# Row moments of odd graph pairs moved from VectorE to ScalarE, and zero matmuls ahead of the first product

## What is computed

```python
h = jnp.maximum(_layernorm(x), 0.0); x = x + relation_layer(h, adj, Wq, Wk, Wv)
h = jnp.maximum(_layernorm(x), 0.0); x = x + graph_attention(h, W, a, beta, adj)
h = jnp.maximum(_layernorm(x), 0.0); x = x + normalised_adj @ (h @ weight) + bias
h = jnp.maximum(_layernorm(x), 0.0); x = x + masked_8_head_attention(h, adj, ...)
def _layernorm(x, eps=1e-05):
    m = mean(x, -1); v = var(x, -1)
    return (x - m) / sqrt(v + eps)
```

## Time and profile before

| | |
|---|---|
| median of 3 runs | 716.94 us (715.76 to 717.35) |
| the profiled execution, its own time | 716.58 us |
| its span in the profile | 714.8 us |
| PE busy | 692.3 us (97%) |
| PEld busy | 652.9 us (91%) |
| DVE busy | 627.9 us (88%) |
| ACT busy | 555.9 us (78%) |
| POOL busy | 462.1 us (65%) |

### The profile page before, as it was taken

The page is one execution under the profiler, slowest core; times in us unless marked ns, Lnnn a source line. Parts: engine busy times, 40 slices in busy tenths (PEclk is TensorE's granted clock), DMA queues, the critical chain, the costliest instruction groups (busy, mean ns, idle before and its releaser), DMA issues.

```text
span 714.8 us, 22548 instructions
## 1 busy us (share of the span) xinstructions
PE 692.3 (97%) x6938; PEld 652.9 (91%) x6938; DVE 627.9 (88%) x2618; ACT 555.9 (78%) x1892; POOL 462.1 (65%) x585
## 2 busy tenths in 40 slices
PE   5999999999999999999998999999999999999996
PEld 5999999999888888889997999999999999999994
DVE  5899888987799999699998999998889998899876
ACT  3665656565689999876665998889888988898895
POOL 2445454554587788588884776776677666766662
DMA  8222310000000000000000000000000000000001
GB/s 246 83 82 89 89 43 0 0 0 2 0 1 2 1 2 1 2 1 0 0 0 1 17 33 17 30 29 30 15 30 29 30 15 30 30 29 16 32 32 45
DMA packets 21710, 20.30 MB, mean 28 GB/s; under 512 B 2449, under 2 KB 21649, under 8 KB 21649
## 3 DMA queue, kind: packets, MB, share of 16 engines
q1 hardware_dynamic: 19456, 18.16, 8.0%
q10 hardware_dynamic: 2192, 1.44, 0.7%
HBM read 11.21 MB, written 8.39 MB: 27 GB/s over the span
## 4 chain that ended last, share of the span: by engine, by line
PE 89%; DVE 3%; ACT 3%; issue 2%; POOL 1%; DMA 1%; POOLq 0%; ACTq 0%; DVEq 0%
PE bank L397 43%; PE bank L1276 8%; PE bank L387 7%; PE bank L166 5%; PE bank L1262 5%; PE bank L1286 4%; PE bank L480 4%; PE bank L837 3%; PE bank L427 3%; PE bank L377 3%; PE bank L461 1%; PE bank L875 1%; PE bank L850 1%; ACT prob L1372 1%; DMA wk<-in_L_gnn_Wk_dram 1%
## 5 line engine op out<-in xcount | busy, mean ns | idle before, releaser
L1372 ACT ACTIVATE prob<-wide,small 128x128 f32<-128x128 f32 x504 | 195.5, 395 | 2.1 <-DVE small L1484 2.1
L1447 POOL TENSOR_TENSOR prob<-prob,small 128x512 f32<-128x512 f32 x127 | 132.3, 1043 | 100.1 <-DVE small L1498 98.1
L1484 DVE CUSTOM_DVE_ANT_0 wide<-bank,mbias 128x128 f32<-128x128 f32 x512 | 115.3, 286 | 0.1
L1372 ACT ACTIVATION_READ_ACCUMULATOR prob<-wide,small 128x1 f32 x504 | 97.2, 193 | 0.0
L155 POOL TENSOR_TENSOR rstd<-vare,mhalf 128x2 f32<-128x2 f32 x104 | 73.3, 704 | 20.5 <-DVE vare L144 20.2
L1276 PE MATMUL bank<-ident,prob 128*128 128x128 f32 x512 | 72.2, 273 | 3.8 <-POOL prob L1447 3.5
L636 POOL TENSOR_TENSOR rnorm<-norm,mhalf 128x2 f32<-128x2 f32 x32 | 22.3, 696 | 81.3 <-ACT relsq L577 81.3
L129 DVE BATCH_NORM_STATS2 stats<-xs 128x6 f32<-128x256 f32 (+1 forms) x176 | 65.6, 415 | 5.9 <-DMA xs<-in_x_dram 5.0
L239 POOL TENSOR_SCALAR xn<-xs,nmean,rstd 128x256 f32<-128x256 f32 x120 | 65.3, 554 | 5.5 <-POOL rstd L155 5.5
L1392 ACT COPY probT<-bank 128x512 f32<-128x512 f32 x96 | 52.3, 580 | 18.7 <-PE bank L1276 18.7
L1276 PEld LDWEIGHTS bank<-ident,prob 128*128 128x128 f32 x512 | 58.3, 140 | 5.5 <-POOL prob L1447 4.8
(11 more groups left out here) (168 smaller groups left out, 1933.1 us busy)
## 6 DMA issues: line engine op xcount, KB each, us to landing
out_dram<-xs SPq DMA_DIRECT2D x31, 256.0 KB, 2.1
xs<-in_x_dram SPq DMA_DIRECT2D x29, 256.0 KB, 2.7
xs<-in_x_dram ACTq DMA_DIRECT2D x1, 512.0 KB, 7.8
xs<-in_x_dram ACTq DMA_DIRECT2D x1, 256.0 KB, 4.3
wq<-in_L_gnn_Wq_dram SPq DMA_DIRECT2D x1, 256.0 KB, 3.9
wk<-in_L_gnn_Wk_dram ACTq DMA_DIRECT2D x1, 256.0 KB, 5.2
wv<-in_L_gnn_Wv_dram SPq DMA_DIRECT2D x1, 256.0 KB, 5.8
w<-in_L_gnn_W_dram SPq DMA_DIRECT2D x1, 256.0 KB, 7.4
```

The costliest lines, as they stand in the source:

```text
L1372: ins = nc.scalar.activation(prob[:, r, i, :], wide[:, r, i, :], ACT.Exp, bias=nmax[r][:, i:i + 1], scale=-1.0, accum_out=rsum[r][:, i:i + 1])
L1447: nc.gpsimd.tensor_tensor(prob[:, r, :, :], prob[:, r, :, :], rinv[r].unsqueeze(2).to_broadcast([128, QUAD, N]), ALU.mult).then_inc(prob_r ...
L1484: nc.vector.tensor_tensor_reduce(out=wide[:, r, i, :], in0=SS[r][:, i * N:(i + 1) * N], in1=mbias[:, :], scale=-1.0, scalar=3e38, op0=ALU. ...
```

## The change

It does four things.

1. The moments of the odd pairs for the second layer are computed on ScalarE by two passes over each graph: `sums_odd` (Identity with scale -1/(16 D) and an accumulator: minus a sixteenth of the mean) and `squares_odd` (Square of x/16 plus that, with an accumulator: the variance). For odd pairs 1 to 29 this is done in the first layer, from step 3 on: the sums in odd steps, the squares in even ones. Pair 31 is done in the second layer, behind ScalarE's step 2.
2. `moments_odd` is gone from VectorE, and the 16 two-column roots of the odd pairs from GpSimd. In their place `root_odd` does eight columns at a time, with two small operations ahead (in the first layer at steps 11, 19 and 27, in the second at step 11).
3. VectorE's first instruction clears 384 columns of `wide`; TensorE then multiplies these zeros six times (twelve passes) into a bank that is written anew later, and only then waits for the first weights.
4. `degrees()` moves behind `normalise(1)`.

```diff
+        def sums_odd(act, i):
+            act.wait_ge(l0_x_done, 2 * i + 2)
+            act.wait_ge(l1_odd_squares, since(i))
+            for g in range(2):
+                ins = nc.scalar.activation(odd_terms[:, g, :], x_of(2 * i + 1, g), ACT.Identity, scale=-1.0 / (16 * D),
+                                           accum_out=mean_odd[:, bass.ds(2 * i + g, 1)])
+            ins.then_inc(l1_odd_sums, 1)
+        def squares_odd(act, i):
+            act.wait_ge(l1_odd_sums, i + 1)
+            for g in range(2):
+                ins = nc.scalar.activation(odd_terms[:, g, :], x_of(2 * i + 1, g), ACT.Square, scale=1.0 / 16,
+                                           bias=mean_odd[:, bass.ds(2 * i + g, 1)], accum_out=var_odd[:, bass.ds(2 * i + g, 1)])
+            ins.then_inc(l1_odd_squares, 1)
-        def root_odd(pool, p):
-            inverse_root(pool, p // 2, l1_stats_ready, l1_rstd_ready, (p // 2) % 2)
+        def root_odd(pool, q):
+            pool.wait_ge(l1_odd_squares, 4 * q + 4)
+            part = slice(8 * q, 8 * q + 8)
+            nc.gpsimd.tensor_scalar(nmean_odd[:, part], mean_odd[:, part], 16.0, None, ALU.mult)
+            nc.gpsimd.tensor_scalar(vare_odd[:, part], var_odd[:, part], EPS, None, ALU.add).then_inc(l1_odd_args, 1)
+            pool.wait_ge(l1_odd_args, q + 1)
+            nc.gpsimd.tensor_tensor(rstd_odd[:, part], vare_odd[:, part], mhalf[:, :], ALU.pow).then_inc(l1_odd_root, 1)
...
+                pe.wait_ge(c_plain, 1)
+                for _ in range(6):
+                    nc.tensor.matmul(OO[:, 0:D], plain[:, 0:128], plain[:, 128:128 + D], start=True, stop=True)
                 pe.wait_ge(qk_loaded, 32)
...
-                def step(p, b):
+                def step(p, b, i=None):
                     copy_t(p)
                     relu_high(p + 1, 1 - b)
                     relation_high(p - 1)
                     squares(p - 1, 1 - b)
+                    if i is not None and b:
+                        sums_odd(act, i)
                     relu_T(p + 1, 1 - b)
+                    if i is not None and not b:
+                        squares_odd(act, i)
                     copy_v(p)
...
+                nc.vector.memset(plain, 0.0).then_inc(c_plain, 1)
                 dve.wait_ge(x_first, 16)
                 statistics(0, 0)
                 normalise(0)
                 statistics(1, 1)
-                degrees()
                 dve.wait_ge(c_high, 1)
...
                 low_part(0, 0)
                 normalise(1)
+                degrees()
...
                 for p in range(PAIRS - 1):
                     step(p)
+                    if p == 2:
+                        sums_odd(act, PAIRS // 2 - 1)
+                        squares_odd(act, PAIRS // 2 - 1)
...
-                    if p + 3 < PAIRS:
-                        if p == 5:
-                            moments_even(dve, PAIRS // 2 - 1)
-                        if p % 2 == 0 and p > 0:
-                            moments_odd(dve, p // 2 + 1, 1)
-                        elif p % 2 and p + 4 < PAIRS:
-                            moments_odd(dve, p // 2 + 2, 0)
+                    if p == 5:
+                        moments_even(dve, PAIRS // 2 - 1)
```

More of the change, by code:

```diff
@@ L73, in gnn_stack_kernel @@
         rstd_even = sb("rstd_even", [128, PAIRS])
+        odd_terms = sb("odd_terms", [128, 2, D])
+        mean_odd = sb("mean_odd", [128, PAIRS])
+        var_odd = sb("var_odd", [128, PAIRS])
+        vare_odd = sb("vare_odd", [128, PAIRS])
+        nmean_odd = sb("nmean_odd", [128, PAIRS])
+        rstd_odd = sb("rstd_odd", [128, PAIRS])
         stats = sb("stats", [128, 4, 2, 6])
@@ L316, in root_even @@
             nc.gpsimd.tensor_tensor(rstd_even[:, part], vare_even[:, part], mhalf[:, :], ALU.pow).then_inc(l1_even_root, 1)
-        def root_odd(pool, p):
-            inverse_root(pool, p // 2, l1_stats_ready, l1_rstd_ready, (p // 2) % 2)
+        def sums_odd(act, i):
[18 more added lines that the diff above has]
+            nc.gpsimd.tensor_tensor(rstd_odd[:, part], vare_odd[:, part], mhalf[:, :], ALU.pow).then_inc(l1_odd_root, 1)
         def centre_first(pool, p, turned, freed):
             if p % 2:
-                b = (p // 2) % 2
-                pool.wait_ge(l1_rstd_ready, p // 2 + 1)
-                scalars = [(nmean[:, b, g:g + 1], rstd[:, b, g:g + 1]) for g in range(2)]
+                pool.wait_ge(l1_odd_root, p // 8 + 1)
+                scalars = [(nmean_odd[:, p - 1 + g:p + g], rstd_odd[:, p - 1 + g:p + g]) for g in range(2)]
             else:
@@ L354, in moments_even @@
                 nc.vector.scalar_tensor_tensor(vare_even[:, part], var, EPS, var, ALU.add, ALU.max).then_inc(l1_even_stats, 1)
[L356 to L370, removed]
         def gather_nodes(pe, ps, p, src, xn_ready):
@@ L618, in _ @@
                 with act.Fori(3, PAIRS // 2 - 1) as j:
-                    step(2 * j + 1, 1)
-                    step(2 * j + 2, 0)
+                    step(2 * j + 1, 1, j - 1)
+                    step(2 * j + 2, 0, j - 1)
                 copy_t(PAIRS - 1)
@@ L661, in _ @@
                         root_even(pool, p // 8 - 1)
+                    if p % 8 == 3 and p > 3:
+                        root_odd(pool, p // 8 - 1)
                 for n in range(2):
                     inverse_norm(PAIRS - 3 + n)
-                    if n % 2:
-                        root_odd(pool, n)
                     centre_first(pool, n, tr_done, PAIRS - 1 + n)
@@ L990, in _ @@
                         root_two(pool, (p - 22) // 6)
-                    if p % 2 and p + 2 < PAIRS:
-                        root_odd(pool, p + 2)
-                    elif p == 8:
+                    if p == 8:
                         root_even(pool, PAIRS // 8 - 1)
+                    if p == 11:
+                        root_odd(pool, PAIRS // 8 - 1)
                     if p >= 2:
```

12 lines of the change are left out of this document (6 added, 6 removed).

## The result

The change is faster: 711.46 us as the median of four runs (711.37 to 711.58), against 716.35 for the kernel before, run beside it four times (715.47 to 717.35). The ratio is 0.9931 [0.9914, 0.9949], 4.9 us less.

What follows compares the result with a forecast made beforehand. The prediction took TensorE's own lost time as the bound; -1.75 (start) + 0.7 (pair 31) - 1.4 - 0.7 (VectorE freed) + 0.3 (`root_odd`) = -2.85 us, giving a median of 714.1 us, range 712.2 to 716.9.

Steps and rivals of the forecast that it cites:

- What bounds the kernel: Whole kernel: TensorE is 97% busy, so only time that TensorE itself loses counts.
- Zeros: Start: zero products raise TensorE's clock before the first product, so `t_product(0)` starts at 10.55, not 12.32; minus 1.75 us.
- The first rival: Start: the clock isn't up in time, the first product still takes near 3.8 us; 715.8 us, chance 0.13.
- `degrees` moved: Start, VectorE: moving it saves the gain's last 0.6 us; the delayed weight remainder stays covered by 0.2; net zero.
- ScalarE in the first layer: Sums (0.85 a pair) and Squares (1.0, or 1.15 with register operations) hide in idle time, cover 1.54 us; zero cost.
- The slower rival: First layer, even steps: Squares exceed the cover and push `copy_v`, 14 steps lose 0.36 each; 719.1 us, chance 0.07.
- Pair 31: Second layer's start: its sums and Squares on ScalarE delay `copy_pT(0)`, and TensorE waits at `attend(0)`; plus 0.7 us.
- `root_odd`: Second layer, step 11, GpSimd: an eight-column power plus 0.4 us for arguments makes `turn`'s weights wait; plus 0.3 us.
- VectorE freed: Second layer: without odd moments seven late `attend`s lose their delay, minus 1.4 us; the last steps gain, minus 0.7.
- The second rival: Second layer: ScalarE, not VectorE, causes the late steps, so only the start gains; 716.2 us, chance 0.14.
- The step that failed: Everything behind the start runs back to back on TensorE, so the gain stays; no term for fourth or steady first layer.
- The third rival: Second layer: the rest of the end's delay, `root_odd`'s 0.3 and L316's 0.36 go too; 712.7 us, chance 0.13.

Runs made afterwards that it cites:

- start_only: The kernel before with only the zeros and the move of `degrees()`; 714.45 us, ratio 0.9980 to the kernel before.
- no_zeros: The changed kernel without the clearing of `wide` and the zero products, `degrees()` still moved; 712.91 us, ratio 0.9957 to the kernel before.
- both_mended: The changed kernel with pair 31's moments on VectorE and `root_odd`'s two small operations a step ahead of its power; 711.15 us, ratio 0.9935 to the kernel before.
- degrees_stay: The changed kernel with `degrees()` back in its old place, ahead of the first weights' remainder; 712.20 us, ratio 0.9948 to the kernel before.
- squares_twice: The changed kernel with each pair of Squares in the first layer's 14 even steps issued twice; 715.53 us, ratio 0.9992 to the kernel before.
- odd_only: The changed kernel without clearing and zeros and with `degrees()` in its old place, leaving the odd moments and their tiles; 713.22 us, ratio 0.9956 to the kernel before.
- tiles_only: The kernel before with the change's six new tiles (2688 bytes per partition) declared and unused; 714.58 us, ratio 0.9978 to the kernel before.
- args_apart: The changed kernel with `root_odd`'s two small operations one step ahead of its power in the second layer; 711.26 us, ratio 0.9930 to the kernel before.
- pad_640: The kernel before with one unused tile of 640 bytes per partition in place of the six; 714.21 us, ratio 0.9978 to the kernel before.

## Why the prediction was right and where it was wrong

**What bounds the kernel: right.** TensorE's own time decides; 30 us less of VectorE's work gave some 1.4 us of the whole.

**Zeros: right, in size too.** I said minus 1.75, from `t_product(0)` at 10.55. It began at 10.15 in the profile after, 2.17 earlier than in the profile before. The surplus is chance: the means are 11.95 over six profiles with the old start and 10.42 over six with the new one, 1.5 apart. start_only gives 1.66 in the median, no_zeros 1.45. Clearing took 0.38 where I took 0.5. The sum has no term for what the first layer gives back, 0.3.

*The first rival* (the clock isn't up in time) exists, in a mild form. With the zeros ahead the product took 1.89 us in the kernel after, 1.93 to 2.00 in five others and 2.30 in both_mended; without them 3.49 to 3.78. The twelve zero passes themselves took 4.24 to 5.49. The Trainium skill, TensorE: Matmul & The Clock Gate, section Part 1 (What's actually happening), says that the moment of the rise differs between runs of one kernel; the traces agree that it differs between executions that begin alike, but in none of seven did the rise come late enough to take all of the gain; in both_mended, the latest, 1.1 of it was left against the 11.96 of the kernel before.

**`degrees` moved: right, a little large.** I said "so the move saves the gain's last 0.6": it was 0.38 between two profiles and 0.5 inside that of degrees_stay. I had taken VectorE to be free at 9.22 for good; the first transfer landed earlier in this execution, and ScalarE's copy bound instead.

**ScalarE in the first layer: right.** Squares at 0.50 each, sums at 0.40 each, as the term had it (0.5 and 0.42). The cover of 1.54 held for 1.0 us of Squares, and squares_twice shows that it ends before 2.0. The slower rival's place was right; its price, the whole excess lost in each of 14 steps, was about twice too high. The Trainium skill, ScalarE: Activation LUTs, section Rules for kernel authors, gives additions and products to VectorE. Taken as a rule for this move, it speaks against it; here the move gained 1.36 (odd_only less tiles_only), as ScalarE's added work fell into its idle time and VectorE's steps had been late.

**Pair 31: right**, plus 0.74 where I said 0.7. **`root_odd`: right in kind**, plus 0.51 where I said 0.3; the power itself is 1.66, but two small operations stand ahead of it and an update of 1.28 between it and the next `xn`, and with the small ones a step earlier (args_apart) the wait is gone. (The roots that went are sixteen, not fifteen.)

**VectorE freed: right in size, in mechanism as far as the runs tell.** Two `attend`s in the chain of the kernel after, in neighbouring steps:

```profile
203.31 0.86 PE bank L856 x4
...
206.80 0.87 PE bank L856 x4
```

Apart from 1.13 at 189.10 (pair 31) and at 284.43 (the end) none in that chain is late. I had minus 1.4 for seven late steps and minus 0.7 for the end. Added up from `product` to `product`, eleven steps of the profile before were longer than 3.49 by 0.09 to 0.30, and none of them is after: minus 2.2; the last step fell from 4.62 to 4.16, minus 0.5. That is minus 2.6 against that one profile. Two of its eleven steps, though, are late in no other profile with the old moments, L316's among them. Against tiles_only it is nine steps, 1.7 us, and 0.5 at the end: minus 2.2, where I had minus 2.1. The parts differ all the same: four steps near the end (3.77, 3.70, 3.68 and 3.79) lost up to 0.3 and not 0.2 each; I had counted late `attend`s, and these show a part of it only. The second rival (ScalarE holds the layer) is out: nearly every step is 3.49 with ScalarE in the same order as before. That it is VectorE's moments and not GpSimd's sixteen small roots whose removal does it is argued from the earlier trace rows and not shown. The end kept 4.16; `normalise_early` (1.08 us on ScalarE from 283.04) still ends right before the `copy_pT` that `attend` waits for at 284.43. I take that as its cause, and no run here took it away.

**The step that failed** is one that stands in the forecast only as an omission: "Everything behind runs on TensorE back to back, so the gain stays", with no term at all for the fourth layer and the steady first one (whose steps it has at 5.11 "as before"; they are 5.09). The six new tiles move every tile declared behind them, and that alone gave 1.5 us, as tiles_only and pad_640 show. With it the sum would have been -4.4. The measured 4.9 us has an interval of 3.7 to 6.2 by its ratio, so the 0.5 that is left can't be told from differences between executions. Nor was 716.94 a typical median of the kernel before: beside the change it was 716.35. From the one the mended sum gives 712.6, inside the range, from the other 712.0. The third rival (more is freed, 712.7) came nearest in time, and that is luck: of its gains, L316's wait was chance in one profile, `root_odd`'s delay stayed, and of the end's wait of 0.88 there is 0.41 left.

The sum after the fact, by the stages of the profiled executions. The last column sets the change against the other profiles with the old start or the old moments, where those differ from the one profile before:

| term | forecast | after against before | against the others |
|---|---|---|---|
| start: zeros and degrees | -1.75 | -2.17 | -1.5 |
| given back in the first layer | no term | +0.3 | +0.3 |
| pair 31 in the second layer | +0.7 | +0.74 | +0.74 |
| late steps and end of the second layer | -2.1 | -2.6 | -2.2 |
| `root_odd` | +0.3 | +0.51 | +0.51 |
| addresses: first and fourth layer | no term | -0.5 and -1.17 | -0.5 and -1.17 |
| sum | -2.85 | -4.9 (span -5.1) | -3.8 |

## What to carry to other kernels

Before an edit that declares a tile is judged, run the old kernel with that tile declared and unused: here a third of the gain came from it, and it would have been credited to the moments. How the later tiles come to lie has to be the same, too, or the test says nothing. Where TensorE waits for its first operands, zeros on it meanwhile let the first product run at the upper clock level; but what comes next (here three small VectorE operations) must be moved aside for all of the gain to arrive. When an engine's late steps are counted, count the steps from one repeated instruction to the next over the whole stage, and not the one instruction in which the delay was first seen; and count them in a second execution, as here two of eleven late steps were in one profile only.

## What the runs showed of the hardware

**Addresses.** Twelve passes of a split product take 1.42 or 1.43 to 1.44 us in the fourth layer, with the same instructions and data. A shift of 640 or of 2688 bytes gave the shorter time, one of 2048 bytes did not; over the kernel it is 1.5 us of 716.

**The clock at the end.** In some executions TensorE's clock falls in the last step, where the engine has gaps. tiles_only, timeline of TensorE, and the row of its windows (length, busy us of each engine, granted clock, DMA):

```profile
700.02 0.66 PE L1282 MATMUL bank<-ident,prob 128*128 128x128 f32 x4 [1.00 <-POOL prob L1453]
701.02 0.66 PE L1282 MATMUL bank<-ident,prob 128*128 128x128 f32 x4 [0.34 <-POOL prob L1453]
702.15 2.90 PE L403 MATMUL bank<-wo,oTs 128*128 128x256 f32 x12 [0.47 <-DVE oTs L1513]
```

```profile
700.00:706.00 6.00, 5.16 (x28) 4.63 (x28) 4.35 (x8) 2.78 (x10) 2.00 (x2) 0.72 0.14 46
```

The product that takes 1.68 us elsewhere takes 2.90 here, after waits of 1.00, 0.34 and 0.47; the mean granted clock of the stretch is 0.72. The kernel after has the same waits at the same place and a clock of 1.00 there, so the same gaps come with the fall and without it. It adds 1.0 to 1.1 us to an execution, more than either mend of the second layer gives. Together with the start, where `t_product(0)` came anywhere from 10.12 to 10.90 in the profiles with zeros, it is why edits of half a microsecond are seen in a stage's time and not in the medians.
